# A vision-transformer layer on one core: the next turn's key and query projections move into the tail of a turn, its value projections, second norm and routing into early attention steps

## What is computed

```
h = patches @ W_proj + b;  h = concat(cls, h)
h = h + attn(layernorm(h))   # 4 expert attentions of 12 heads, sliding window 64,
                             # then silu(fused @ w_gate) * (fused @ w_up)
h = h + ffn(layernorm(h))    # per token one of 4 experts (argmax), gelu, hidden size 768
```

## Time and profile before

| | us |
|---|---|
| median of 3 runs | 4499.01 |
| lowest and highest | 4497.68, 4499.13 |
| the profiled execution | 4497.74 |
| its span, first to last instruction | 4495.9 |

### The profile page before, as it was taken

One profiled execution on the slowest core, in us unless ns is written; L12 is line 12 of the kernel. 1 busy time (PEld: TensorE's weight loads), 2 busy tenths in 40 slices (PEclk: granted clock), 3 DMA queues, 4 the chain that ended last, 5 costly groups with the idle time before them and its releaser, 6 DMA issues. The chain is left out here.

```text
span 4495.9 us, 119008 instructions
## 1 busy us (share of the span) xinstructions
PE 3880.3 (86%) x41326; PEld 2852.4 (63%) x41326; DVE 3491.9 (78%) x9633; ACT 3028.6 (67%) x9620; POOL 1091.6 (24%) x1496
## 2 busy tenths in 40 slices
PE   3888888888888898888888888888888888886998
PEld 2666666666666666666666666666666666664776
DVE  4888877787888888777778888887777788885665
ACT  2777766676777777676667777776667677772333
POOL 0222222222222222222222222222222222221222
PEclk7999999999999999999999999999999999997999
DMA  5122221111111222211111112222111111125664
GB/s 180 42 49 51 50 50 48 46 46 44 46 29 47 50 51 50 50 48 45 45 46 46 29 46 50 51 50 50 47 45 46 46 44 30 46 50 178 204 214 155
DMA packets 254292, 285.69 MB, mean 64 GB/s; under 512 B 69289, under 2 KB 236755, under 8 KB 244098
## 3 DMA queue, kind: packets, MB, share of 16 engines
q1 hardware_dynamic: 230242, 210.41, 18.4%
q10 hardware_dynamic: 4608, 38.73, 2.8%
q0 software_dynamic: 18912, 29.35, 1.9%
HBM read 123.49 MB, written 39.28 MB: 36 GB/s over the span
## 5 line engine op out<-in xcount | busy, mean ns | idle before, releaser
L864 ACT ACTIVATE p_s<-bank,smin 128x128 f32<-128x128 f32 (+1 forms) x6144 | 1821.6, 375 | 183.2 <-DVE smin L945 163.5
L945 DVE TENSOR_REDUCE smin<-bank 128x3 f32<-128x384 f32 (+1 forms) x2048 | 1135.5, 554 | 218.2 <-PE bank L721 189.7
L741 PE MATMUL bank<-ident_s,p_s 128*128 128x128 f32 (+1 forms) x6144 | 884.1, 253 | 28.2 <-DVE pt_f L950 7.9
L716 PE MATMUL bank<-masks_s,mask_id_s 128*128 128x384 f16 (+1 forms) x2048 | 675.3, 330 | 30.7 <-DVE qt_f L916 16.4
L741 PEld LDWEIGHTS bank<-ident_s,p_s 128*128 128x128 f32 (+1 forms) x6144 | 601.6, 142 | 138.9 <-issue 103.5
L721 PE MATMUL bank<-stacks_f 128*128 128x256 f16 (+3 forms) x4096 | 679.9, 247 | 0.0
L891 POOL TENSOR_TENSOR w_s<-o_raw 128x192 f32<-128x192 f32 (+1 forms) x512 | 306.9, 599 | 1180.1 <-DVE o_raw L938 1180.1
L249 PE MATMUL bank<-zt,wqkv_s 128*128 128x394 f16 x1920 | 411.0, 378 | 170.8 <-PEq L1008 161.5
L950 DVE TENSOR_TENSOR pt_f<-bank,pt_f 128x384 f16<-128x384 f32 x1024 | 552.7, 540 | 0.0
L855 ACT CAST pt_f<-bank 128x384 f16<-128x384 f32 x1024 | 510.8, 499 | 0.0
L721 PEld LDWEIGHTS bank<-stacks_f 128*128 128x128 f16 (+1 forms) x4096 | 431.1, 105 | 123.1
(11 more groups left out here) (130 smaller groups left out, 6283.5 us busy)
## 6 DMA issues: line engine op xcount, KB each, us to landing
stacks_f<-qt_f SPq DMA_DIRECT2D x768, 73.9 KB, 2.1
stacks_f<-kt_f SPq DMA_DIRECT2D x1536, 36.9 KB, 2.1
wx_t<-wx_d SPq DMA_DIRECT2D x36, 1344.0 KB
x_raw<-x_t_dram ACTq DMA_DIRECT2D x32, 1182.0 KB
rec_t<-rec_d SPq DMA_DIRECT2D x36, 582.0 KB, 3.9
stacks_f<-w_dram SPq DMA_DIRECT2D x2, 1536.0 KB
wx_d<-w_s SPq DMA_DIRECT2D x8, 384.0 KB
v_f<-v_f SPq DMA_DIRECT2D x192, 4.1 KB
```

The lines of the kernel that those rows point to most:

```text
L716: nc.tensor.matmul(ps, mask_id_s[:, 0:rows], masks_s[:, m0:m0 + HU * kn], start=True, stop=False)
L741: mm = nc.tensor.transpose(turned[:, j * rows:j * rows + rows], p_slot(u)[:, k0:k0 + 128], ident_s[0:rows, 0:rows])
L864: ins = nc.scalar.activation(p_slot(s)[:, j * kn:j * kn + kn], bank[s % SR][0:rows, j * kn:j * kn + kn], ACT.Exp, scale=-1.0, bias=smin[0: ...
L945: nc.vector.tensor_reduce(least, ps, AX_X, ALU.min).then_inc(S["min_ready"], 1)
```

## The change

A turn now begins with its scores. The twelve key and query projections of the *next* turn are made in the tail (once in the second block, for the first turn), with the first stack of queries and keys. The eight value projections are made in steps 0 to 6 of attention; the second layernorm in steps 1 to 15, the routing in steps 15 to 19. The patch products move from step 0 to step 21. The first layernorm of the next pair moves from the tail to steps 40 to 58. The attention output `ot` gets storage of its own (it shared that of the queries). In the tail ACT copies the raw image between the output copies and the rest of the projections, and POOL makes its low part after all divisions. Helpers (`turn`, `high_of`, `low_of`) now do one of two blocks at a time.

Constants of the schedule (steps, and the PSUM bank of each projection):

```diff
+        proj = [("v", j) for j in (0, 2, 1, 3, 4, 6, 5, 7)] + qk
+        NV = 8
+        PROJ_BANK = [3, 4, 5, 6, 7, 6, 7, 7] + [4, 5, 4, 5, 4, 5, 6, 4, 5, 6, 4, 5]
...
-        PATCH_STEP, PATCH_GAP, PATCH_LAG, PATCH_RATE = 0, 2, 1, 2
-
-        GU_STEPS = {64: 0, 69: 1, 70: 2, 74: 3}
-        LN_STEPS = (70, 74)
...
+        V_STEPS = {0: (0, 1), 1: (2, 3), 2: (4,), 3: (5,), 4: (6,), 6: (7,)}
+
+        Z2_MOMENTS, Z2_NORMS = {1: 0, 2: 1, 3: 2, 4: 3}, {6: (0, 1), 7: (2, 3)}
+        Z2_TURNS, AT_LOGITS, AT_CHOOSE, AT_COUNT, AT_PLACE = {9: 0, 12: 1}, 15, 16, 18, 19
+        PATCH_STEP, PATCH_GAP, PATCH_LAG, PATCH_RATE = 21, 2, 1, 2
+
+        OT_STEPS = {41: 0, 44: 1, 47: 2}
+        OT_HI, OT_LO = 1, 2
+        Z1_MOMENTS, Z1_NORMS, Z1_TURNS = {40: 0, 42: 1, 44: 2, 46: 3}, {49: (0, 1), 50: (2, 3)}, {52: 0, 56: 1}
+
+        GU_STEPS, PROJ_STEPS = {64: 0, 65: 1, 67: 2}, {66: NV}
```

The new helpers of a projection (`first` is 8 only in the second block):

```diff
+        def project_in(pe, n):
...
+            product(proj_psum(n), passes).then_inc(S["proj_mm"], 1)
+
+        def project_hi(act, n, first=0):
+
+            act.wait_ge(S["proj_mm"], n - first + 1)
+            nc.scalar.activation(proj_target(n, 0), proj_src(n), ACT.Copy, scale=proj_scale(n)
+                                 ).then_inc(S["proj_hi"], 1)
+
+        def project_lo(dve, n, first=0):
+
+            dve.wait_ge(S["proj_hi"], n - first + 1)
...
+                                           ).then_inc(S["proj_lo"], 1)
```

PE, in a step (between the scores of unit s and the patches, the transposes of unit s-2 and the values of unit s-5) and in the tail:

```diff
                     for s in range(PIPE):
                         if s < UNITS:
                             scores(s)
+                        for n in V_STEPS.get(s, ()):
+                            before = [m for m in range(n) if PROJ_BANK[m] == PROJ_BANK[n]]
+                            if before:
+                                pe.wait_ge(S["proj_lo"], before[-1] + 1)
+                            project_in(pe, n)
+                        if s in Z2_TURNS:
+                            if Z2_TURNS[s] == 0:
+                                pe.wait_ge(S["proj_lo"], NV)
+                            else:
+                                pe.wait_ge(S["z2t_lo"], 1)
+                            turn(pe, z2, "z2_ready", OT_BANK, Z2_TURNS[s], "z2t_mm")
+                        if s == AT_LOGITS:
+                            pe.wait_ge(S["z2t_lo"], 2)
+                            logits(OT_BANK)
...
+                    project_next(NV + 1)
+                    gate_first(3)
+                    pe.wait_ge(S["z1t_lo"], 2)
+                    turn_o(1, 0)
+                    turn_o(1, 1)
+                    project_next(NV + 2)
+                    pe.wait_ge(S["ot_lo"], 4)
+                    turn_o(1, 2)
+                    for n in range(NV + 3, NV + 6):
+                        project_next(n)
+                    for tt in range(4):
+                        for b in range(OB // 2, OB):
...
+                            mm = gate_up(tt, b)
+                        mm.then_inc(S["gu_mm"], 1)
+                        project_next(NV + 6 + tt)
+                    project_next(NV + 10)
+                    project_next(NV + 11)
```

ACT, in a step (after the exponentials of unit s) and in the tail:

```diff
+                        for n in V_STEPS.get(s, ()):
+                            project_hi(act, n)
...
+                    project_hi(act, NV + 2)
+                    ot_high(1, 2)
+                    act.wait_ge(S["patch_mm"], 4)
+                    act.wait_ge(x_in, 16 * i + 48)
+                    nc.scalar.copy(x_s[:, 0], x_raw).then_inc(S["x_hi"], 1)
+                    for n in range(NV + 3, NV + 6):
+                        project_hi(act, n)
                     for tt in range(4):
...
+                        squash(tt)
+                        project_hi(act, NV + 6 + tt)
```

VectorE, in a step (after the minimum of unit s and the low part of unit s-4):

```diff
+                        for n in V_STEPS.get(s, ()):
+                            project_lo(dve, n)
...
+                        if s in Z2_MOMENTS:
+                            moments(chain, h, Z2_MOMENTS[s])
+                        for tt in Z2_NORMS.get(s, ()):
+                            normalise(dve, 0, h, z2, "z2_ready", tt)
```

SP, at the end of a turn:

```diff
+                    sp.wait_ge(S["proj_lo"], NV + 2 * HP)
+                    sp.wait_ge(S["scores_mm"], UNITS)
+                    stack_queries(sp, 0, "stacked_next")
+                    stack_keys(sp, 0, "stacked_next")
+                    sp.wait_ge(S["stacked_next"], 16 * 9)
```

More of the change, by code:

```diff
@@ L166, in vit_layer @@
         XR, PR = 3, 4
+        OT_AT = PR * 2 * PT2 + XR * 256
         p_s = sb1("p_s", [128, XR * HU * KWN[1]])
@@ L269, in patch_part, with turn, high_of, low_of @@
                 mm.then_inc(S["patch_mm"], 1)
-        def turn(pe, z, ready, b0, done):
+        def turn(pe, z, ready, b, blk, done):
+            f0, fn = Z_BLOCKS[blk]
             for tt in range(4):
                 _, _, c0, rows = tile_of(tt)
-                if ready:
+                if blk == 0:
                     pe.wait_ge(S[ready], tt + 1)
[L277 to L280, removed]
+                mm = nc.tensor.transpose(bank[b][0:fn, c0:c0 + rows], z[0:rows, tt, f0:f0 + fn],
+                                         ident_s[0:rows, 0:rows])
             mm.then_inc(S[done], 1)
[L283 to L294, removed]
+        def high_of(act, b, blk, target, done, his):
+            fn = Z_BLOCKS[blk][1]
+            act.wait_ge(S[done], blk + 1)
+            nc.scalar.copy(target[0:fn, 2 * blk, 0:TP], bank[b][0:fn, 0:TP]).then_inc(S[his], 1)
+        def low_of(dve, b, blk, target, his, los):
+            fn = Z_BLOCKS[blk][1]
+            dve.wait_ge(S[his], blk + 1)
+            low = target[:, 1, 0:TP] if blk == 0 else target[128 - fn:128, 2, 0:TP]
+            nc.vector.tensor_tensor(low, bank[b][0:fn, 0:TP], target[0:fn, 2 * blk, 0:TP], ALU.subtract
+                                    ).then_inc(S[los], 1)
         class Chain:
@@ L846, in _, with ot_high, squash @@
-                    act.wait_ge(S["x_lo"], 1)
-                    act.dma_start(x_raw, x_t[(i + 2) % STEPS]).then_inc(x_in, 16)
-                    for s in range(PIPE):
+                    def ot_high(e, blk):
+                        act.wait_ge(S["ot_mm"], 3 * e + blk + 1)
+                        nc.scalar.copy(ot[:, 3 * e + blk, 0, :], ot_bank(e, blk)[:, 0:TP]).then_inc(S["ot_hi"], 1)
+                    def squash(tt):
+                        rows = tile_of(tt)[3]
+                        act.wait_ge(S["gu_mm"], tt + 1)
+                        nc.scalar.activation(sig[0:rows, tt, :], bank[GU_BANKS[tt]][0:rows, 0:D], ACT.Tanh,
+                                             scale=0.5 * INV).then_inc(S["sig_ready"], 1)
@@ L849, in _ @@
+                    for s in range(UNITS + LAG_HI):
                         u = s - LAG_HI
@@ new lines, in _ @@
+                    project_lo(dve, NV + 1)
+                    ot_low(1, 0)
+                    ot_low(1, 1)
+                    project_lo(dve, NV + 2)
+                    ot_low(1, 2)
+                    for n in range(NV + 3, NV + 6):
+                        project_lo(dve, n)
+                    for tt in range(4):
+                        residual(tt)
+                        project_lo(dve, NV + 6 + tt)
+                    project_lo(dve, NV + 10)
+                    project_lo(dve, NV + 11)
@@ L1039, in _ @@
                     normalise(dve, 0, h, z2, "z2_ready", tt)
-                low_of(dve, 6, zt2, "z2t_hi", "z2t_lo")
-                choose(dve, chain)
+                for blk in range(2):
+                    low_of(dve, 6 + blk, blk, zt2, "z2t_hi", "z2t_lo")
+                choose(dve, chain, 6)
                 place(dve, chain)
```

426 lines of the change are left out of this document (215 added, 211 removed).

## The result

| | before | after |
|---|---|---|
| median, us | 4498.77 | 4817.22 |
| ratio, 95% interval | | 1.0707, 1.0689 to 1.0726 |
| span of the profiled execution | 4495.9 | 4813.0 |
| mean granted TensorE clock | 0.952 | 0.912 |

The change adds 318 us; 279 were forecast, and 4778 us for the run. In the changed kernel a turn is best cut at its 64 minima (L1032, one in each step). The mean of 31 turns, from first minimum to first minimum, is 133.09 us, against 123.7 before.

The account below looks back on a forecast made before the run. ACT and VectorE were taken to bound attention, PE's products, handovers and the close the rest. 21.1 + 75.8 + 32.9 + 1.0 = 130.8 against 122.55 a turn, 279 us with the beginning, gives 4778 us; range 4530 to 4910.

Parts of the forecast that it names:

- Part 1: Rest of the turn, last score to next first score: gets shorter, 32.9 us against 46.74.
- The wait behind the image copy: Tail: PE waits for NV+3's low part, whose high part stands behind ACT's 2.15 us image copy; 2.1 us.
- Part 2: First eight attention steps, with the value projections: get longer, 21.1 us against 8.80.
- the loop: Attention steps with a value projection: minimum, exponentials, high part, low part wait in turn; 2.37 us, second projection adds 0.48.
- Part 3: Other 56 attention steps, with patches, norms and routing: 75.8 us against 66.2, between 72.5 and 79.
- the two waits: Steps 12 and 15: PE waits for VectorE's low part of the step before; 0.55 us each, 1.1 together.
- Part 4: Lower TensorE clock after the gap at the turn's start, 1.0 us a turn; longer beginning, 15 us once.
- low clock: Rival, chance 0.12: PE at 0.50 in first eight steps and tail; turn 135.5 us, total time 4929 us.
- the reference turn: The turn of the kernel before that the forecast costed against: 75.81 first to last score plus 46.74, 122.55 us.
- The beginning: Once, before the first turn: second block gets twelve projections ahead of its memsets; 15 us, from 10 to 20.
- Half the loop: Rival, chance 0.09: next minimum finds scores ready, first eight steps cost 17 instead of 21.1; total time 4588 us.
- Interleaving pays: Rival, chance 0.15: ACT and VectorE fill each other's waits; first eight 13.5, others 73.5, rest 31.5; faster, 4400 us.

Follow-up runs that it names:

- e5_image_early: Changed kernel with only ACT's raw image copy moved ahead of the tail's first key projection; 4724.84 us.
- e1_low_later: Changed kernel with VectorE making each value projection's low part one step later, behind the next minimum; 4615.33 us.
- e2_high_first: Changed kernel with ACT making the value projections' high parts ahead of the step's exponentials; 4701.60 us.
- e8_norm: Changed kernel with the image copy early and the second norm's moments and normalisations in the tail; low parts in their old steps; 4701.28 us.
- e6_three: Changed kernel with three edits: low parts one step later, PE's second-norm transposes, logits and count behind the step's own transposes and value products, image copy early; 4487.68 us.
- e11_norm_two_spread: e7_three_and_norm with two value products at turn's end, banks re-dealt, last normalisations before last low parts, last two value projections a step later; 4433.26 us.
- e7_three_and_norm: e6_three with the second norm's moments and normalisations in the tail and gate products one projection earlier; 4486.68 us.
- e9_two_at_end: e6_three with the first two value projections' products made at the end of the turn before and banks re-dealt; 4526.01 us.

## Why the prediction was right, and where its sizes were off

**Part 1, the rest of the turn.** Right. 32.9 was put on it from last to first score; from last to first minimum it is 32.03 at full clock (from last to first score too) and 33.41 in the mean. The wait behind the image copy was 1.97 (2.1 forecast), in the place and by the chain described, and e5_image_early shows that it was on the path. Unforeseen was that merely delaying the copy gives its time to a residual addition.

**Part 2, the first eight steps.** Right, step by step: forecast 2.85, 3.45, 2.97, 2.97, 2.97, 1.1, 3.1, 1.7; in the turn of the first stretch above 3.71, 3.44, 3.06, 2.97, 3.06, 1.02, 3.17, 1.59. Only step 0 is off, at a clock of 0.55; where it runs at full clock, as in the turn of the third stretch above, it is 2.85, and that turn's 21.15 meets the sum of 21.1. Steps 1 to 4 take 12.5 us in every turn of after, at clocks from 0.89 to 0.99, so the lower clock is not what makes them long. That the loop is the cause is shown by two cuts (e1_low_later, e2_high_first) and by the bare loop of e8_norm.

**Part 3, the other 56 steps.** The mean is 78.05 against 75.8. The excess lies in steps 8 to 23 and goes with the lower clock. Stretches of after, steps 8 to 15 and 16 to 23:

```profile
1459.61:1472.34 12.73, 11.42 (x138) 9.64 (x138) 9.74 (x27) 10.04 (x35) 2.22 (x4) 0.77 0.14 30
1472.34:1485.62 13.28, 11.71 (x143) 9.87 (x142) 10.75 (x40) 9.00 (x32) 4.38 (x5) 0.75 0.20 55
```

At clocks of 0.93 and 0.86 the same work took 11.25 and 12.57 (e5_image_early, above). With these two instead of 12.73 and 13.28, the other eights at 10.12, 9.92, 12.49, 10.89 and the last seven steps at 8.55, the part is 75.8, the forecast; one turn of after (first minimum at 2236.62) does take 75.83. Steps 8 to 15 take 10.89 at full clock in e1_low_later; steps 16 to 23 ran at 0.87 or less in every turn of every changed kernel, so what they take at full clock no run shows. Inside it the terms were not all right: steps 24 to 39, with nine steps of patches, take 20.04, 1.6 more than steady attention, where the forecast's 1.6 for six steps would make 2.4; the two waits measured 0.9 instead of 1.1.

**Part 4, the clock, is the term that was mis-sized:** 1.0 us a turn. From the least disturbed pieces of a turn, 21.15, 75.8 and 32.03, a turn would be 129.0; the mean is 133.09, so some 4.1 us a turn go with the lower clock: 0.5 in the first eight steps, 2.2 in the other 56, 1.4 in the rest. The forecast's 1.0 looked for it only behind the new gap at the turn's start, where the 0.5 lie. It also falls in the tail (35.30 at 0.90 against 32.03 at 1.00, with 3.27 us more of busy PE) and in steps 8 to 23. The rival *low clock* was thus half right: its turn was 135.5, the forecast's 130.8, and 133.09 came. The total came nearer than the turn by luck: the reference turn of 122.55 is 1.15 shorter than the mean of before, which made the forecast loss larger and took back half of the 2.3 us that the turn was short by.

**The beginning.** Before, the first turn began with its projections at 91.28; after, it begins with its scores at 105.59. So the block ahead of it is 14.3 us longer; 15 was forecast. What was moved without a price (scatters, the stack of group 1) shows in no step: the interval from step 7 to 8 is 1.59, 1.7 forecast, and the next one 1.30.

**The rivals.** *Half the loop*: wrong for this change; it forecast 17 for the first eight steps, and 21.63 came. *Interleaving pays*: wrong for this order of instructions, as the first eight steps are above its 16.5 and the run is slower. With three waits taken out and all of the interleaving kept, it pays 0.25% (e6_three). The 1.45% of e11_norm_two_spread, with 12.34, 76.46 and 32.41 where the rival's bounds were 13.5, 73.5 and 31.5, came with a part of it taken back: the second norm is out of the attention steps again, and two value products are made at the turn's end. The Trainium skill's "Perfetto Trace Analysis", section "Optimization Strategy", says that interleaving stretches with different most contended engines may improve the time. The traces of this case agree in the end, but only with the mutual wait and the queued waits taken out: as first ordered, the interleaved kernel is 7.1% slower.

**What stays open.** Why a stretch at the lower clock falls in one turn's tail and in the next turn's steps 8 to 23. Small edits move it: in e11_norm_two_spread turns alternate between some 122.0 and 120.3, one with 33.2 in the rest, the other with 31.6. No kernel here changed the clock alone.

## What to carry to other kernels

Before moving work into a stretch where two engines are busy 91%, write down the order of the instructions in one step on both: if A makes x, B makes y behind x, A finishes y and only then makes the next x, the step costs the sum of both engines' work, and busy shares don't show it. Let the finishing half slip one step behind, so that it finds its input ready; here that one line gave back 202 of 318 us. And after each edit look what is queued behind the new wait: two of the edits tried here (the later image copy, the re-dealt banks) put in a wait about as long as what they took out.

## What was not expected of the hardware

- A VectorE addition with both inputs in SBUF took 3.82 us instead of 0.36, beside a POOL subtraction of 4.67 that had begun 1.06 us before it, and ended just behind it. VectorE's low parts, with one input in PSUM, take 0.57 beside the same POOL operation in the changed kernel (1553.49, POOL from 1553.14 for 4.68).
- The mean granted clock differs between kernels that do the same work in another order: 0.912 in the changed kernel, and 0.949 to 0.952 in five of the six kernels with the three edits (0.936 in the sixth), as in the kernel before. The length of the gap in PE's products ahead of a turn's scores does not tell by itself what follows. In after it is 3.1 to 3.2 us ahead of all 31 turns that follow another, and step 0 runs at 1.00 in 17 of them and at 0.54 to 0.66 in 14; in e7_three_and_norm it is 3.7 us, with 0.61 to 0.63 in every step 0 behind it. With a gap of 2.0 us, step 0 runs at 1.00 in all 31 such turns of e11_norm_two_spread, but at 0.50 in 10 of the 31 of e9_two_at_end.
